# An integer softmax whose rounded quotient is made by two ScalarE passes in place of one ScalarE and one VectorE pass

## The reference, as far as it matters

```python
x_int = x / scale
x_int = x_int - jnp.max(x_int, axis=-1, keepdims=True)
...
exp_int = jnp.maximum(jnp.floor(z * jnp.exp2(n - q)), 0.0)
exp_sum = jnp.sum(exp_int, axis=-1, keepdims=True)
ratio = jnp.round(exp_sum / jnp.maximum(exp_int, 1.0))
big = jnp.floor(jnp.log2(ratio))
big = big + jnp.where(ratio - jnp.exp2(big) >= jnp.exp2(big - 1.0), 1.0, 0.0)
out = jnp.exp2(-jnp.clip(big, 0.0, qmax - 1.0))
```

## Time and profile before

| what | value |
|---|---|
| median of three timed runs | 2543.01 us (2528.36 to 2548.34) |
| the profiled execution, its own time | 2521.54 us |
| span from its first to its last instruction | 2519.8 us |
| busy over the span | PE 1665.8 us, DVE 1449.6 us, ACT 1108.1 us, POOL 335.1 us |
| mean granted TensorE clock | 0.796 of full speed |

### The profile page before, as it was taken

One profiled execution on the slowest core, in us unless ns is written; L12 is line 12 of the kernel. 1 busy time (PEld: TensorE's weight loads), 2 busy tenths in 40 slices (PEclk: granted clock), 3 DMA queues, 4 the chain that ended last, 5 costly groups with the idle time before them and its releaser, 6 DMA issues. The chain is left out here.

```text
span 2519.8 us, 35593 instructions
## 1 busy us (share of the span) xinstructions
PE 1665.8 (66%) x11734; PEld 1360.9 (54%) x11734; DVE 1449.6 (58%) x2801; ACT 1108.1 (44%) x2159; POOL 335.1 (13%) x417
## 2 busy tenths in 40 slices
PE   3688979747804577756598833323498299459994
PEld 2366658546603344354597433222387299459994
DVE  6598961341178899868323679999614411443223
ACT  4466742303335688752021438887322155312221
POOL 0000000036500000000242000000000142024431
PEclk9798969868856788886699866555699599779997
DMA  3200010324420000003375000000003354437674
GB/s 84 64 18 17 21 25 1 92 58 140 138 80 1 7 6 5 2 1 107 123 220 169 21 4 5 4 5 1 12 1 89 95 179 148 135 109 226 220 213 163
DMA packets 137067, 189.55 MB, mean 75 GB/s; under 512 B 51581, under 2 KB 111133, under 8 KB 136893
## 3 DMA queue, kind: packets, MB, share of 16 engines
q1 hardware_dynamic: 118977, 148.83, 19.3%
q0 software_dynamic: 15360, 36.72, 5.0%
q10 hardware_dynamic: 2556, 1.77, 0.3%
HBM read 149.99 MB, written 33.68 MB: 73 GB/s over the span
## 5 line engine op out<-in xcount | busy, mean ns | idle before, releaser
L989 DVE TENSOR_TENSOR 40_l3f_mlp_hidden<-40_l3f_mlp_gate,40_l3f_mlp_first 128x512 f32<-128x512 f32 x51 | 35.1, 688 | 184.4 <-ACT 40_l3f_mlp_gate L967 106.4
L2500 PE MATMUL 14_pla_line<-14_pla_low,ident 128*128 128x435 f32 x96 | 68.1, 876 | 62.0 <-ACT 14_pla_low L2550 62.0
L2703 PE MATMUL 29_log_int_turned<-identb,29_log_int_ratio 128*87 128x128 bf16 x272 | 32.7, 315 | 107.4 <-DVE 29_log_int_ratio L3238 107.4
L1202 PE MATMUL 2_performer_p_u<-perf_proj,2_performer_yT 128*87 128x512 f32 (+1 forms) x204 | 96.5, 618 | 10.6 <-DVE 2_performer_arg L1363 9.4
L1005 DVE TENSOR_SCALAR 9_l0f_mlp_y<-9_l0f_mlp_second,l0f_routing_weight 128x192 f32<-128x192 f32 x51 | 21.0, 417 | 141.6 <-remote 65.1
L882 PE MATMUL 40_l3f_mlp_first<-40_l3f_mlp_xT,40_l3f_mlp_w 128*128 128x128 f32 x816 | 101.4, 278 | 0.6 <-issue 0.6
L882 PEld LDWEIGHTS 40_l3f_mlp_first<-40_l3f_mlp_xT,40_l3f_mlp_w 128*128 128x128 f32 x816 | 96.9, 195 | 0.8 <-issue 0.8
L967 ACT ACTIVATE 40_l3f_mlp_gate<-40_l3f_mlp_first 128x512 f32<-128x512 f32 x51 | 30.5, 597 | 135.3 <-PE 40_l3f_mlp_first L887 126.6
L2703 PEld LDWEIGHTS 29_log_int_turned<-identb,29_log_int_ratio 128*87 128x87 bf16 x272 | 29.2, 193 | 109.0 <-DVE 29_log_int_ratio L3238 109.0
L1003 DVE TENSOR_TENSOR 36_l3a_mlp_y<-36_l3a_mlp_second,l3a_experts_b_rows 128x192 f32<-128x192 f32 x29 | 10.4, 358 | 132.8 <-issue 94.3
L2714 PE MATMUL 29_log_int_p_out<-l2a_vb,29_log_int_wT 87*87 87x16 bf16 x384 | 30.9, 222 | 84.3 <-ACT 29_log_int_wT L3160 84.3
(11 more groups left out here) (903 smaller groups left out, 5165.1 us busy)
## 6 DMA issues: line engine op xcount, KB each, us to landing
40_l3f_mlp_w<-in_L_ffn_w_dram SPq DMA_DIRECT2D x51, 768.0 KB
25_l1f_mlp_w<-in_L_ffn_w_dram SPq DMA_DIRECT2D x29, 768.0 KB
36_l3a_mlp_w<-in_L_attn_W_dram SPq DMA_DIRECT2D x29, 576.0 KB
9_l0f_mlp_w<-in_L_ffn_down_w_dram SPq DMA_DIRECT2D x51, 192.0 KB
l3a_experts_w<-in_L_attn_W_dram SPq DMA_DIRECT2D x8, 576.0 KB, 8.3
l1a_blocks<-l1a_qkb SPq DMA_DIRECT2D x192, 5.4 KB, 1.8
l1f_experts_w<-in_L_ffn_w_dram SPq DMA_DIRECT2D x8, 384.0 KB
l2a_blocks<-l2a_qkb SPq DMA_DIRECT2D x192, 5.4 KB, 1.8
```

The source lines that it names most:

```text
L989: v.tensor_tensor(hidden[j % 2][:], gate[j % 2][:], first[j % 2][1][:, 0, 0:HT, :], ALU.mult).then_inc(hidden_done, 1)
L1202: ins = t.matmul(p_u[:, k, 0:(EIGHT - h) * M], yT[b % 2][:, k, :], proj[:, h:EIGHT, :].rearrange("p h m -> p (h m)"), start=True, stop=True)
L2500: nc.tensor.matmul(to_w[:, n], kit.ident[:], of_w[:, n], start=start, stop=stop)
L2703: ins = nc.tensor.transpose(turned[:, n // 8, (n % 8) * 128:(n % 8 + 1) * 128], w[:, n * NT:(n + 1) * NT], kit.identb[:])
```

## The change

Line numbers of the changed kernel lie up to two above those of the kernel before.

```diff
-        raw, quo, power = (kit.sb(ctx, n, [128, UW], I32) for n in ("raw", "quo", "power"))
+        raw, quo, power, whole = (kit.sb(ctx, n, [128, UW], I32) for n in ("raw", "quo", "power", "whole"))
...
                     act.wait_ge(ratio_ready, i + 1)
+                    a(whole[:], guess[:], ACT.Copy).then_inc(rounded, 1)
                     if i >= 2:
                         act.wait_ge(turned_done, i - 1)
-                    a(ratio[i % 2][:], guess[:], ACT.Identity, bias=bias[:, 0:1]).then_inc(rounded, 1)
+                    act.wait_ge(rounded, i + 1)
+                    a(ratio[i % 2][:], whole[:], ACT.Copy, scale=LIFT).then_inc(scaled, 1)
...
             def weights(j):
                 r = ratio[j % 2]
-                dve.wait_ge(rounded, j + 1)
-                v.tensor_scalar(r[:], r[:], -MAGIC, LIFT, ALU.add, ALU.mult).then_inc(scaled, 1)
                 dve.wait_ge(scaled, j + 1)
...
                 if j < U:
                     exponential(j)
+                if j < U:
+                    sum_up(j)
                 if 0 <= i < U:
                     weights(i)
-                if j < U:
-                    sum_up(j)
```

## The result

| | kernel before | changed kernel |
|---|---|---|
| median of ten executions each | 2523.16 us (2514.45 to 2548.34) | 2510.34 us (2508.03 to 2521.36) |
| profiled execution, span | 2519.8 us | 2507.2 us |
| stage 29, from its first DVE instruction to that of stage 30 | 295.86 us | 284.75 us |
| exponential to exponential in the steady stretch | 17.21 us | 16.37 us |

The ratio of the times is 0.9948, with a 95% interval of 0.9925 to 0.9971: the changed kernel is 0.5% faster, some 13 us, and the interval (7 to 19 us) lies clear of zero. A ratio in this document is the one on record, worked out from the single executions; it isn't the quotient of the two medians beside it and can differ from it by up to 0.15%. The median of the kernel before is now that of ten executions. The first three of them, 2543.01, 2548.34 and 2528.36 us, were the three slowest of the ten.

The account below looks back on a forecast made before the run. DVE was taken to set the pace, at 17.21 us per unit. First interval 0.45, 13 intervals 10.8, less tail 0.72, gave 10.5 us; 2543.0 - 10.5 = 2532.5 us, range 2516 to 2549.

Parts of the forecast that it names:

- cycle of DVE: Exponential to exponential on DVE, one unit: 17.21 - 0.95 + 0.12 = 16.38 us, a gain of 0.83 us.
- new ACT passes: The two 128x1479 passes on ACT replacing rounding and DVE scaling: 1.53 us each, ends 1.44 and twice 1.53.
- bit operation: DVE reaches it at E + 3.54, E being the unit's exponential start on DVE; 0.60 us to spare.
- cover at the tops: Next unit's tops done on ACT at E + 4.76, cut by DVE at E + 4.91: 0.15 us, the thinnest cover.
- ACT idle per unit: ACT's spare time in each unit falls from 2.99 to 0.60 us, so ACT doesn't become the bound.
- first interval: First units, no store between bit operation and tops: DVE waits for tops until E + 4.76, gaining 0.45 us.
- tail: Stage end after the last exponential, where nothing covers ACT: a loss of 0.12 + 0.60 = 0.72 us.
- The dependent pair: On DVE, the sum directly follows the exponential it reads: 1.73 us instead of 1.61, adding 0.12 us.
- Rival 1: Tops come late in stage 29 and ACT's chain sets the pace: time 2536, from 2534.5 to 2538.5 us; chance 15%.
- Rival 2: Int32 to float takes a double pass on ACT, so slower than before: 2553 or 2576 us; chance 3%.
- Rival 3: Stages behind give the gain back, by a transfer or PE clock: time 2543 us; chance 7%.
- Rival 4: In the stage, dependent pair free and no wait at the tops: gain 12.8 us, time 2530 us; chance 5%.

Follow-up runs that it names:

- the extra pass: Changed kernel plus one unused 512-column ACT pass between scaling pass and read-out of the scores: cycle 16.62 us, stage 289.10 us, 4.35 longer than the changed kernel's.
- the store on ACT: Changed kernel with the product's store moved from DVE to ACT behind Exp: stage 281.36 us; 2514.02 us against 2524.99 of the kernel before, ratio 0.9968.
- the seventh: Changed kernel plus an unused 512-column ACT pass, next tops between the new ACT passes, bit operation behind the next clip: cycle 16.82 us, stage 291.43 us.

## Why the prediction was right in the stage and wrong in the time

The time was 2510.34 us, under the range of 2516 to 2549. The change itself did what was forecast, so the two are taken apart.

**The level: the step that failed.** The words are: "the median, 2543.01, is what a timing is compared with, so I predict 2543.0 - 10.5 = 2532.5 us." The gain was set on the median of three runs, although the profiled execution, one more sample of the same kernel, lay 21.5 us under it. Ten executions put the kernel before at 2523.16. The other line of the same step, 2521.54 - 10.5 = 2511.0, was 0.7 us off; that it came so close is luck in part, since the executions of one kernel spread over more than 10 us. The range failed for the same reason: its lower end was that median less the gain and less some 16 us for the spread, as if the three executions had lain evenly around the middle. They were the upper part of a skewed distribution: two of the three are 20 and 25 us above 2523, which is the size of the steps seen above, 21 us in stage 18 and some 20 to 25 in three of the thirteen. That those two executions had such a step is likely, not shown: they left neither a trace nor a clock. The three were also taken ahead of the other seven, and whether that had a part in it stays open. With 16 in 80, an estimate is that two or more of any three are of this kind about one time in ten (one in nineteen with the 5 in 36 of the kernel before), so the sample was bad luck, and taking it for the level the mistake. The chance given to a time under 2517.6 us, 8%, was for luck of this kind.

**The gain: mechanism right, size 0.6 us short.** Forecast 10.5 us, in the stage 11.1, by the timed medians 12.8 and 9.8 (by the recorded ratios 13 and 6). By terms:

| term | forecast | measured |
|---|---|---|
| cycle of DVE | 16.38 us | 16.37 us |
| sum behind the exponential it reads | 1.73 us | 1.72 us |
| new ACT passes | 1.53 us each (1.44 as the end) | 1.42 and 1.44 us |
| starts: first to second, second to next | 1.56, 1.42 us | 1.51, 1.34 us |
| bit operation | E + 3.54 | E + 3.54 |
| cover at the tops | 0.15 us | about 0.3 us |
| ACT idle per unit | 0.60 us | 0.71 us |
| first interval | gain 0.45 us | gain 0.63 us |
| intervals behind it | 13 x 0.83 = 10.8 us | 10.94 us |
| tail | loss 0.72 us | loss 0.46 us |

The term that was sized wrong is the new passes on ACT, for which the rows offered 1.44 and 1.53 us and the higher was taken, by what is converted. What decided was how the scale and bias are given. The quotient L3152 and the new L3174 are the same function on the same types and shape, and differ in the scale alone, which L3152 reads from a tile: 1527 and 1419 ns, means of 16. The prediction also said that no row has int32 in and float out. The shown rows have none, but the trace of the kernel before has such a pass in stage 14, with the time that the second new pass then took (groups of instructions: busy time of all in us, mean of one in ns, idle time before):

```profile
L2542 ACT ACTIVATE 14_pla_fall<-14_pla_count 128x1479 f32<-128x1479 int32 x16 | 23.0, 1437 | 0.5
```

By the figures of the Trainium skill, ScalarE: Activation LUTs, section What ACT_TABLE_LOAD costs, 1418 ns was the estimate for each new pass, and the trace agrees (1419 and 1437 ns). In the steady stretch it made no difference, since the cover held either way; in the first interval and the tail, where nothing covers ACT, the forecast was 0.2 and 0.3 us too low, which fits the shorter passes.

**The dependent pair.** The forecast took 0.12 us from the two rows of before and set aside the statement of the Trainium skill, VectorE: DVE Perf Modes, section The DRAIN you can't avoid, that "the semaphore costs nothing extra here". Two runs bear the forecast out, +0.12 us (17.21 to 17.33) and -0.13 us (16.37 to 16.24) per unit. For passes of 1479 elements the pair costs something.

**The rivals.** Rival 1, the tops come late: not in the changed kernel, where the cover was 0.3 us; both runs that used it up (the extra pass, the store on ACT) show exactly this wait, so the place was rightly named. Rival 2, a double pass for int32: 1.44 us, fallen. Rival 3, the stages behind give it back: the stage's gain of 11.1 stands beside 12.8 and 9.8 in the times, so that no loss of the whole gain is seen, but their intervals would also hold a few us given back. One place is open. Stage 36, which streams weights, took 150.8 us in the one trace of the kernel before that is in the slower group of stage 9, and 155.8 and 154.8 in the two traces with the changed stage there; in the other group it took 149 in all. Whether 4 or 5 us are given back on such a chip, three traces don't decide. Rival 4, more than forecast: 11.1 is between it and the forecast, but not for its reason. The prediction also said that the exponential of the last unit would start 11 us sooner after the first: it was 11.57 (255.35 to 243.78).

## What to carry to other kernels

When work moves from the bounding engine to one with idle time, write down for each consumer when it wants the result and when it gets it, in starts from one fixed point of the cycle. Here the same move was worth -4 us or +11 us, depending on one line of order, and ACT's idle time of 0.71 us in each unit didn't keep a pass of 0.52 us from costing 0.25. Counted by places, the cycle came out within 0.05 us of the forecast in six of seven kernels; the seventh is the one with PE's turn left out. Include the engines that look free (PE's turn of the weights was the one I missed in my own variant). And where a handful of times lies well off the profiled execution, ask which of them is the sample that isn't typical, and let the range hold both.

## What the runs showed that I had not expected

- The same program had 2523 to 2525 us in some sets and 2478 to 2482 in others, each taken on one chip; two thirds of the difference stand in stage 9, where the DMA engines moved 135 or 164 GB/s for the same work.
- In one of eleven traces PE's granted clock stayed at 0.50 through stage 18, and the stage took 61.6 us where it takes 40.5. What PE did in the 50 us ahead was the same as in the first trace of the kernel before, where the clock rose (27.0 and 26.9 us busy, clock 0.77 in both). What tips it is open.
- ACT passes of 128x1479 with immediate scale and bias took 1.42 to 1.44 us and those with a scale or bias from a tile 1.51 to 1.53, whichever of float and int32 they read and wrote.
